# First cross attention of a two-layer block: scores by row halves of the feature axis, the maximum subtracted by VectorE, one low part by GpSimd, and a new order on every engine

## The chip, the cores and the metric

The kernel runs on one core of one Trainium2 chip. The metric is the device time of one execution in microseconds (us); a quoted time of the kernel is the median of several executions. What is shown as a row comes from one profiled execution. PE is TensorE's matmul stream and PEld its weight loads, DVE is VectorE, ACT is ScalarE, POOL is GpSimd and SP is SyncE.

## The reference, cut to what matters

The input `x` holds 64 examples of 128 tokens by 128 features, and every example has a context of 77 tokens. Two layers follow each other; each is a cross attention to the context and then a mixture of experts with 8 experts, and both parts are added to `x` times a gate. Only the first attention concerns the change. Its heads have 8 features, and a feature map makes 16 out of them:

```python
def _feature_map(x, fm_w, fm_b):
    z = jnp.einsum('nshd,ed->nshe', x, fm_w) + fm_b
    return jnp.concatenate([jnp.exp(z), jnp.exp(-z)], axis=-1)
v, k, q = (_feature_map(x, fm_w, fm_b) for x in (v, k, q))
scores = jnp.einsum('nqhd,nkhd->nhqk', q, k) / jnp.sqrt(jnp.float32(EMBED))
attn = jax.nn.softmax(scores, axis=-1)
out = jnp.einsum('nhql,nlhd->nqhd', attn, v)
out = out.reshape(N, S, HEADS * EXP_DIM)
return out @ fc_w.T + fc_b
```

The queries are the layer-normalized `x`, keys and values are the context, and there are 16 heads.

## The kernel before, in words

`flamingo_kernel` runs its stages one behind the other, with a barrier between them: loading `x` (it stays in SBUF as `x_all`), the constants of the layer norm, the first attention (`feature_attention`, the stage a0), router and experts of layer 0, the second attention (`relative_attention`, written in the same way), and router and experts of layer 1. The change is in `feature_attention` and in the call of `layernorm_constants` ahead of it.

In `feature_attention` every engine runs a loop over slots, one slot for one example n, and a slot holds steps of neighbouring examples: while the scores of example n are made, the probabilities of n-1 are multiplied with the values, and n-2 and n-3 are finished. The function `slot` of each engine is the order, written out by hand; the engines meet only at semaphores. `slots` (L62) writes the first and last slots out and loops over the middle ones, two slots in a pass.

The steps of an example, with the lines of the kernel before:

- `normalize` (L420, DVE) makes the normalized rows `a_xn`, `prep_turn` (L222, PE) transposes them, `copy_xn` (L323, ACT) copies them beside the context in `a_xc`; `prep_z` (L228, PE) and `features` (L329, ACT, the exponential) make `a_feat`, whose 256 features lie in two halves c of 128 partitions, 8 heads in each.
- POOL (L393) writes `a_kfeat`: the 77 keys of a half c eight times over, each time with all but one head's 16 partitions at zero. So one matmul over 128 partitions gives the scores of four heads, and the other heads add nothing. `add_bias` is POOL's third instruction (L401).
- A quarter u is four heads. `scores` (L248, PE) makes its 128 x 308 scores in one of two PSUM banks, in float32. `row_max` (L426, DVE) takes the maximum of each head. For quarters 0 to 2, `shift_by_max` (L432, DVE) scales the four maxima, and `exp` (L342, ACT) runs four activations, one for a head, out of PSUM with that bias. For quarter 3 (`ON_DVE`), DVE subtracts the maxima from all 308 columns (L437) and one activation follows (L346).
- `turn` (L258, PE) transposes the four heads into PSUM, `high_prob` (L354, ACT) copies them as float16, and `low_prob` (L445, DVE) subtracts that copy from the PSUM values, which leaves the low part. `mix` (L267, PE) multiplies high and low parts with the values, 12 small matmuls for a quarter. `prep_value`, `high_value` and `low_value` make the two parts of the values.
- `inverse_sum` and `divide` (DVE), `fin_turn` (PE), `copy_mixed` (ACT), `fin_project` (PE), `residual` and `statistics` (DVE) finish an example.

Two places of the code matter for the waits. The first is that `scores` waits until ACT has read the bank (L252), the second that the DVE's scaling of the maxima has SBUF on both sides:

```python
wait(pe, exped, 4 * n + u - 1)
nc.tensor.matmul(score_ps[u % 2][:, 0:QW], feat[p][:, c, 0:P],
                 kfeat[p][:, c, 4 * (u % 2):4 * (u % 2) + 4, :],
...
nc.vector.tensor_scalar(shift[u][:, :], top[u][:, :], -SCALE, None,
                        ALU.mult).then_inc(shift_ready, 1)
```

## Time and profile before

| What | Value |
| --- | --- |
| Median of 3 runs | 2408.27 us (2404.83 to 2421.33) |
| The profiled execution | 2413.15 us |
| Its span, first to last instruction | 2411.4 us |
| Mean granted TensorE clock | 0.944 of full speed |
| PE, DVE, ACT, POOL busy over the span | 92%, 86%, 67%, 64% |

The profiled execution took 4.88 us more than the median of the runs, and its span leaves 1.75 us of it outside. The stage a0 is a fifth of the span, from 31 to 534 us. A row of a timeline says when an instruction or a run of equal ones (x2, x4) starts, how long it lasts, and in brackets how long the engine sat idle before it and what it then waited for. An engine starts its next instruction before the last one has ended for good, so the time that an instruction takes out of an engine's slot is the distance from start to start, a little less than the length shown.

### The profile page before, as it was taken

How to read it: one execution, taken by the hardware profiler on the slowest of the kernel's cores; microseconds unless marked ns; L12 is line 12 of the kernel's file. 1: busy time of each engine (PE TensorE's matmuls, PEld its weight loads, DVE VectorE, ACT ScalarE, POOL GpSimd, SP SyncE). 2: the span in 40 equal slices, each digit the busy share in tenths (PEclk: the TensorE clock that was granted, in tenths of full speed). 3: DMA queues.
4: the chain of work that ended last, by engine and by line, in shares of the span. 5: the costliest groups of instructions: out<-in, count | busy, mean ns of one | idle time of the engine just before them, and what ended most of it. 6: DMA issues, size and time to landing. Idle time of an engine off the chain costs nothing. (4 is left out here: it accounts for less than half of the span.)

```text
span 2411.4 us, 83171 instructions
## 1 busy us (share of the span) xinstructions
PE 2227.9 (92%) x28294; PEld 1764.3 (73%) x28294; DVE 2070.8 (86%) x4625; ACT 1610.1 (67%) x3917; POOL 1534.7 (64%) x1166
## 2 busy tenths in 40 slices
PE   4999999978879999999999399999999986899999
PEld 3888888865546666666666299999999976566666
DVE  6999999987878888888889588888888878888888
ACT  4888888863345555565565377777777753688887
POOL 2333333324446666666666499999999953688888
PEclk9999999995589999999999699999999985899999
DMA  2000000003052222222221345555555530000000
GB/s 80 6 5 5 5 5 5 5 4 69 0 112 83 84 83 80 85 78 90 75 90 54 86 80 75 83 74 81 77 79 78 77 55 35 6 13 13 13 13 13
DMA packets 476806, 123.92 MB, mean 51 GB/s; under 512 B 431731, under 2 KB 446707, under 8 KB 475968
## 3 DMA queue, kind: packets, MB, share of 16 engines
q1 hardware_dynamic: 344352, 89.38, 17.5%
q10 hardware_dynamic: 132384, 33.63, 6.3%
q8 instruction: 41, 0.67, 0.1%
q14 instruction: 29, 0.24, 0.0%
HBM read 109.03 MB, written 13.89 MB: 51 GB/s over the span
## 5 line engine op out<-in xcount | busy, mean ns | idle before, releaser
L1086 POOL TENSOR_TENSOR f_low<-f_hidden,f_high 128x512 f16<-128x512 f32 x336 | 442.3, 1322 | 250.1 <-ACT f_high L1021 248.1
L1044 DVE TENSOR_TENSOR f_hidden<-f_hidden,f_share 128x512 f32<-128x512 f32 x336 | 374.2, 1114 | 0.0
L398 POOL TENSOR_TENSOR a_kfeat<-a_feat,a_head_mask 128x616 f32<-128x616 f32 x128 | 153.7, 1221 | 312.2 <-ACT a_feat L333 312.2
L1230 POOL TENSOR_TENSOR f_low<-f_hidden,f_high 128x512 f16<-128x512 f32 x256 | 296.6, 1159 | 70.9 <-ACT f_high L1173 70.5
L1027 ACT ACTIVATE f_act_out<-f_gate 128x512 f32<-128x512 f32 x336 | 200.4, 596 | 194.8 <-PE f_gate L991 194.8
L1067 DVE SCALAR_TENSOR_TENSOR f_hidden<-f_up,f_act_out 128x512 f32<-128x512 f32 x336 | 229.8, 684 | 82.8 <-PE f_up L991 59.6
L1615 POOL TENSOR_TENSOR a_q_head_high<-a_q_t_high,a_head_mask 128x2048 f16<-128x2048 f16 x64 | 233.0, 3640 | 56.2 <-PE a_score L1417 48.2
L1021 ACT ACTIVATE f_high<-f_hidden 128x512 f16<-128x512 f32 x336 | 210.5, 627 | 72.7 <-DVE f_hidden L1044 71.3
L1001 PE MATMUL f_y<-w_down_high,f_high 128*128 128x128 f16 x1344 | 242.6, 220 | 2.2 <-POOL f_low L1086 2.2
L1001 PE MATMUL f_y<-w_down_high,f_low 128*128 128x128 f16 x1344 | 242.6, 219 | 0.0
L1001 PE MATMUL f_y<-w_down_low,f_high 128*128 128x128 f16 x1344 | 242.5, 219 | 0.0
L1615 POOL TENSOR_TENSOR a_q_head_low<-a_q_t_low,a_head_mask 128x2048 f16<-128x2048 f16 x64 | 232.8, 3638 | 0.0
L1216 DVE SCALAR_TENSOR_TENSOR f_hidden<-f_in,f_act_out 128x512 f32<-128x512 f32 x256 | 175.7, 686 | 50.2 <-ACT f_act_out L1180 50.2
L1557 ACT ACTIVATE a_prob_t_high<-a_trans 77x512 f16<-77x512 f32 x256 | 151.6, 592 | 94.0 <-PE a_trans L1426 88.5
L350 ACT ACTIVATE a_prob<-a_score,a_shift 128x77 f32<-128x77 f32 x768 | 185.4, 327 | 40.4 <-DVE a_shift L442 32.9
L1180 ACT ACTIVATE f_act_out<-f_in 128x512 f32<-128x512 f32 x256 | 152.8, 597 | 76.2 <-PE f_in L1142 70.6
L254 PE MATMUL a_score<-a_kfeat,a_feat 128*128 128x308 f32 x512 | 192.2, 458 | 6.1 <-ACT a_prob L350 1.5
L1718 DVE TENSOR_TENSOR a_prob_t_low<-a_trans,a_prob_t_high 77x512 f16<-77x512 f32 x256 | 175.0, 684 | 17.7 <-ACT a_prob_t_high L1557 6.0
L1415 PE MATMUL a_score<-a_k_t_high,a_q_head_high 128*128 128x77 f16 x1024 | 186.5, 201 | 2.8 <-POOL a_q_head_low L1615 2.8
L1417 PE MATMUL a_score<-a_key_table_low,a_q_pos 128*128 128x77 f16 x1024 | 186.8, 202 | 0.0
L1417 PE MATMUL a_score<-a_key_table_high,a_q_pos 128*128 128x77 f16 x1024 | 186.7, 202 | 0.0
L1154 PE MATMUL f_y<-w_high,f_high 128*128 128x128 f16 x1024 | 184.9, 220 | 1.8 <-DVE x_all L1194 0.5
(264 smaller groups left out, 9025.0 us busy)
## 6 DMA issues: line engine op xcount, KB each, us to landing
f_share<-expert_shares SPq DMA_DIRECT2D x128, 256.0 KB, 3.1
a_q_pos<-queries ACTq DMA_DIRECT2D x64, 512.0 KB, 4.2
f_share<-expert_shares SPq DMA_DIRECT2D x128, 128.0 KB, 3.0
relative_values<-a_rel_all SPq DMA_DIRECT2D x512, 8.0 KB, 1.7
x_all<-in_x SPq DMA_DIRECT2D x4, 1024.0 KB, 8.0
f_share<-expert_shares SPq DMA_DIRECT2D x128, 32.0 KB, 1.8
queries<-a_q_parts SPq DMA_DIRECT2D x64, 64.0 KB, 4.3
a_rel<-relative_values SPq DMA_DIRECT2D x64, 64.0 KB, 3.6
```

The lines of the kernel that those rows point to most:

```text
L254: nc.tensor.matmul(score_ps[u % 2][:, 0:QW], feat[p][:, c, 0:P], kfeat[p][:, c, 4 * (u % 2):4 * (u % 2) + 4, :], start=True, stop=True).th ...
L350: last = nc.scalar.activation(prob[u][:, h, :], score_ps[u % 2][:, KC * h:KC * (h + 1)], ACT.Exp, bias=shift[u][:, h:h + 1], scale=SCALE)
L1001: mm = nc.tensor.matmul(dst, h[r][:, own], w_down[part][:, m, :], start=(m == 0 and t == 0 and k == 0), stop=(m == M - 1 and k == 2), skip ...
L1021: nc.scalar.activation(high[r][:, :], hidden[r][:, :], ACT.Copy).then_inc(high_ready, 1)
L1027: nc.scalar.activation(act_out[m % RING][:, :], gate_ps[m % BANKS][:, :], ACT.Silu, scale=1.0 / WSCALE).then_inc(act_ready, 1)
L1044: nc.vector.tensor_tensor(hidden[r][:, :], hidden[r][:, :], share[k][:, :, :].rearrange("p t q -> p (t q)"), ALU.mult).then_inc(scaled, 1)
L1067: nc.vector.scalar_tensor_tensor(out=hidden[r][:, :], in0=up_ps[m % BANKS][:, :], scalar=1.0 / WSCALE, in1=act_out[r][:, :], op0=ALU.mult, ...
L1086: nc.gpsimd.tensor_tensor(low[r][:, :], hidden[r][:, :], high[r][:, :], ALU.subtract).then_inc(low_ready, 1)
L1230: nc.gpsimd.tensor_tensor(low[k][:, :], hidden[k][:, :], high[k][:, :], ALU.subtract).then_inc(low_ready, 1)
L1415: nc.tensor.matmul(dst, q[:, QC * g:QC * (g + 1), :], t[:, :], start=(k == 0), stop=False)
L1417: mm = nc.tensor.matmul(dst, q_pos[p][:, g, :], key_table[k][:, 0, window], start=False, stop=(k == 1))
L1615: nc.gpsimd.tensor_tensor(q_head[p][k][:, :, :], q_t[p][k][:, :].unsqueeze(2).broadcast_to([P, P, NH]), head_mask[:, :].unsqueeze(1).broad ...
```

## The change

- **Row halves.** `scores` takes a half c instead of a quarter u. For each of the two halves r of the partitions (0 to 63 and 64 to 127, four heads in each) it issues one matmul over 64 partitions, into bank r; u is 2c + r. `a_kfeat` needs the keys four times instead of eight, with a mask `own_mask` that is the sum of the two halves of the old one.
- **Maximum.** For all four quarters DVE subtracts the maxima out of PSUM into `a_prob` (`subtract_max`), and `exp` is one activation of 128 x 308 from SBUF to SBUF. The scaling of the maxima and `shift` are gone. `scores` now waits for the subtraction (`shifted`), not for the exponential.
- **Normalizing** goes from DVE to ACT (`normalize`, scale and bias from `xn_shift`, which `layernorm_constants` now makes with one more DVE instruction).
- **Low part of quarter 3.** ACT copies the transposed quarter 3 once more, as float32, to `prob_3` (`whole_prob`), and POOL subtracts the float16 copy from it (`low_prob` on POOL). DVE keeps the other three.
- **Order.** The slot of each engine is written anew. `turn` of quarter 1 now waits for `whole_prob` and `high_prob` of quarter 3, `mix` of quarter 3 for POOL and moves to the next slot; `mask_keys` of POOL runs one example ahead and stands behind POOL's `low_prob`; `prep_turn` and `fin_turn` move from the last part of a slot to the first part of the next.

The diff, cut to its core:

```diff
-                def scores(n, p, u):
-                    if inside(n, 0, B):
-                        if u % 2 == 0:
-                            pe.wait_ge(kfeat_ready, 2 * n + u // 2 + 1)
-                        wait(pe, exped, 4 * n + u - 1)
-                        c = u // 2
-                        nc.tensor.matmul(score_ps[u % 2][:, 0:QW], feat[p][:, c, 0:P],
-                                         kfeat[p][:, c, 4 * (u % 2):4 * (u % 2) + 4, :],
-                                         start=True, stop=True).then_inc(score_ready, 1)
+                def scores(n, p, c):
+                    if inside(n, 0, B):
+                        pe.wait_ge(kfeat_ready, 2 * n + c + 1)
+                        wait(pe, shifted, 4 * n + 2 * c)
+                        for r in range(2):
+                            own = slice(HALF * r, HALF * (r + 1))
+                            nc.tensor.matmul(score_ps[r][:, 0:QW], feat[p][own, c, 0:P], kfeat[p][own, c, :, :],
+                                             start=True, stop=True).then_inc(score_ready, 1)
 
                 def turn(n, u):
                     if inside(n, 0, B):
                         pe.wait_ge(exped, 4 * n + u + 1)
-                        wait(pe, prob_low, 4 * n + u - 1)
+                        if u == 1:
+                            wait(pe, prob_3_whole, n)
+                            wait(pe, prob_high, 4 * n)
+                        else:
+                            wait(pe, prob_low, 3 * n + max(u - 1, 0))
...
                 def mix(n, p, u):
                     if inside(n, 0, B):
-                        pe.wait_ge(prob_low, 4 * n + u + 1)
+                        if u == 3:
+                            pe.wait_ge(prob_3_low, n + 1)
+                        else:
+                            pe.wait_ge(prob_low, 3 * n + u + 1)
...
                 def slot(n, p):
                     o = 1 - p
+                    mix(n - 2, p, 3)
                     scores(n, p, 0)
+                    prep_turn(n + 1, o)
+                    fin_turn(n - 3, o)
                     turn(n - 1, 2)
+                    turn(n - 1, 3)
                     prep_z(n + 1, o)
-                    mix(n - 1, o, 0)
                     fin_project(n - 3, o)
                     scores(n, p, 1)
-                    turn(n - 1, 3)
+                    mix(n - 1, o, 0)
+                    turn(n, 0)
                     prep_value(n, p)
                     mix(n - 1, o, 1)
-                    scores(n, p, 2)
-                    turn(n, 0)
+                    turn(n, 1)
                     mix(n - 1, o, 2)
-                    fin_turn(n - 2, p)
-                    prep_turn(n + 2, p)
-                    scores(n, p, 3)
-                    turn(n, 1)
-                    mix(n - 1, o, 3)
...
                 def exp(n, u):
                     if inside(n, 0, B):
-                        act.wait_ge(shift_ready, 4 * n + u + 1)
-                        if u in ON_DVE:
-                            last = nc.scalar.activation(prob[u][:, :, :], prob[u][:, :, :], ACT.Exp, scale=SCALE)
-                        else:
-                            wait(act, prob_ready, 4 * n + u - 3)
-                            for h in range(HQ):
-                                last = nc.scalar.activation(prob[u][:, h, :], score_ps[u % 2][:, KC * h:KC * (h + 1)],
-                                                            ACT.Exp, bias=shift[u][:, h:h + 1], scale=SCALE)
-                        last.then_inc(exped, 1)
+                        act.wait_ge(shifted, 4 * n + u + 1)
+                        nc.scalar.activation(prob[u][:, :, :], prob[u][:, :, :], ACT.Exp, scale=SCALE).then_inc(exped, 1)
...
+                def whole_prob(n):
+                    if inside(n, 0, B):
+                        act.wait_ge(prob_ready, 4 * n + 4)
+                        wait(act, prob_3_low, n)
+                        nc.scalar.activation(prob_3[:, :, :],
+                                             trans_ps[1][0:KC, :].rearrange("k (h q) -> k h q", h=HQ),
+                                             ACT.Copy).then_inc(prob_3_whole, 1)
...
+                def normalize(n, p):
+                    if inside(n, 0, B):
+                        wait(act, xn_t, n - 1)
+                        nc.scalar.activation(xn[p][:, :], x_all[:, n, :], ACT.Identity, bias=xn_shift[:, n, :],
+                                             scale=rstd[:, n, :]).then_inc(xn_ready, 1)
+
                 def slot(n, p):
                     o = 1 - p
+                    exp(n - 1, 3)
+                    copy_xn(n + 1, o)
+                    normalize(n + 3, o)
+                    copy_mixed(n - 3, o)
                     high_prob(n - 1, 2)
+                    exp(n, 0)
+                    whole_prob(n - 1)
+                    high_prob(n - 1, 3)
                     features(n + 1, o)
-                    exp(n, 0)
-                    high_prob(n - 1, 3)
+                    exp(n, 1)
                     high_value(n, p)
-                    exp(n, 1)
                     high_prob(n, 0)
+                    high_prob(n, 1)
                     exp(n, 2)
-                    copy_xn(n + 2, p)
-                    high_prob(n, 1)
-                    copy_mixed(n - 2, p)
-                    exp(n, 3)
...
+                def low_prob(n):
+                    if inside(n, 0, B):
+                        pool.wait_ge(prob_3_whole, n + 1)
+                        pool.wait_ge(prob_high, 4 * n + 4)
+                        nc.gpsimd.tensor_tensor(prob_t[3][1][:, :, :], prob_3[:, :, :], prob_t[3][0][:, :, :],
+                                                ALU.subtract).then_inc(prob_3_low, 1)
+
+                def mask_keys(n, p):
                     if inside(n, 0, B):
                         pool.wait_ge(feat_ready, n + 1)
                         wait(pool, score_ready, 4 * n - 4)
                         for c in range(2):
                             nc.gpsimd.tensor_tensor(
-                                kfeat[p][:, c, :, :], feat[p][:, c, P:P + KC].unsqueeze(1).broadcast_to([P, 8, KC]),
-                                head_mask[:, :].unsqueeze(2).broadcast_to([P, 8, KC]), ALU.mult).then_inc(kfeat_ready, 1)
+                                kfeat[p][:, c, :, :], feat[p][:, c, P:P + KC].unsqueeze(1).broadcast_to([P, HQ, KC]),
+                                own_mask[:, :].unsqueeze(2).broadcast_to([P, HQ, KC]), ALU.mult).then_inc(kfeat_ready, 1)
+
+                def add_bias(n):
+                    if inside(n, 0, B):
                         nc.gpsimd.tensor_tensor(x_all[:, n, :], x_all[:, n, :], fc_b[:, :],
                                                 ALU.add).then_inc(x_biased, 1)
 
-                pool.wait_ge(weights_ready, 4)
-                slots(pool, 0, LO, HI, B, slot)
+                def slot(n, p):
+                    low_prob(n - 1)
+                    mask_keys(n + 1, 1 - p)
+                    add_bias(n)
...
-                def shift_by_max(n, u):
-                    if inside(n, 0, B):
+                def subtract_max(n, u):
+                    if inside(n, 0, B):
+                        s = score_ps[u % 2][:, 0:QW].rearrange("q (h k) -> q h k", h=HQ)
                         dve.wait_ge(top_ready, 4 * n + u + 1)
-                        if u in ON_DVE:
-                            wait(dve, prob_ready, 4 * n + u - 3)
-                            nc.vector.tensor_tensor(
-                                prob[u][:, :, :], score_ps[u % 2][:, 0:QW].rearrange("q (h k) -> q h k", h=HQ),
-                                top[u][:, :].unsqueeze(2).broadcast_to([P, HQ, KC]), ALU.subtract).then_inc(shift_ready, 1)
-                        else:
-                            wait(dve, exped, 4 * n + u - 3)
-                            nc.vector.tensor_scalar(shift[u][:, :], top[u][:, :], -SCALE, None,
-                                                    ALU.mult).then_inc(shift_ready, 1)
+                        wait(dve, prob_ready, 4 * n + u - 3)
+                        nc.vector.tensor_tensor(prob[u][:, :, :], s, top[u][:, :].unsqueeze(2).broadcast_to([P, HQ, KC]),
+                                                ALU.subtract).then_inc(shifted, 1)
...
                 def slot(n, p):
                     o = 1 - p
                     row_max(n, 0)
+                    row_max(n, 1)
+                    subtract_max(n, 0)
+                    subtract_max(n, 1)
                     inverse_sum(n - 2, p)
-                    shift_by_max(n, 0)
                     low_prob(n - 1, 2)
                     divide(n - 2, p)
-                    row_max(n, 1)
                     residual(n - 3)
-                    shift_by_max(n, 1)
-                    low_prob(n - 1, 3)
-                    low_value(n, p)
                     row_max(n, 2)
                     statistics(n - 3)
-                    shift_by_max(n, 2)
+                    row_max(n, 3)
+                    subtract_max(n, 2)
+                    subtract_max(n, 3)
+                    low_value(n, p)
                     low_prob(n, 0)
-                    row_max(n, 3)
-                    normalize(n + 3, o)
-                    shift_by_max(n, 3)
                     low_prob(n, 1)
...
-        layernorm_constants(nc, "ln0", stats, mean[:, :, 0], rstd[:, :, 0], B)
-        feature_attention(nc, B, io, x_all, stats, mean, rstd, ident, gates)
+        layernorm_constants(nc, "ln0", stats, mean[:, :, 0], rstd[:, :, 0], B, xn_shift[:, :, 0])
+        feature_attention(nc, B, io, x_all, stats, mean, rstd, xn_shift, ident, gates)
```

What the new order looks like is seen best on DVE and PE. First DVE, where the rows begin a slot that is written out (example 3, ahead of the loop); `a0_score0` and `a0_score1` are the two banks, the number behind `a0_top`, `a0_shift`, `a0_prob` and `a0_prob_t` is the quarter. Before:

```order
L430 TENSOR_REDUCE a0_top0<-a0_score0 128x4
L464 RECIPROCAL a0_rden1<-a0_mix1 128x16
L442 TENSOR_SCALAR a0_shift0<-a0_top0 128x4
L449 TENSOR_TENSOR a0_prob_t2_low<-a0_trans0,a0_prob_t2_high 77x512
L471 TENSOR_TENSOR a0_mixed1<-a0_mix1,a0_rden1 128x256
L430 TENSOR_REDUCE a0_top1<-a0_score1 128x4
L479 TENSOR_TENSOR x_all<-x_all,a0_fin 128x128
L442 TENSOR_SCALAR a0_shift1<-a0_top1 128x4
L449 TENSOR_TENSOR a0_prob_t3_low<-a0_trans1,a0_prob_t3_high 77x512
L456 SCALAR_TENSOR_TENSOR a0_vfeat1_low<-a0_prep,a0_vfeat1_high 77x16x16
L430 TENSOR_REDUCE a0_top2<-a0_score0 128x4
L485 BN_STATS stats<-x_all 128x6
```

And now:

```order
L455 TENSOR_REDUCE a0_top0<-a0_score0 128x4
L455 TENSOR_REDUCE a0_top1<-a0_score1 128x4
L462 TENSOR_TENSOR a0_prob0<-a0_score0,a0_top0 128x308
L462 TENSOR_TENSOR a0_prob1<-a0_score1,a0_top1 128x308
L484 RECIPROCAL a0_rden1<-a0_mix1 128x16
L469 TENSOR_TENSOR a0_prob_t2_low<-a0_trans0,a0_prob_t2_high 77x512
L491 TENSOR_TENSOR a0_mixed1<-a0_mix1,a0_rden1 128x256
L499 TENSOR_TENSOR x_all<-x_all,a0_fin 128x128
L455 TENSOR_REDUCE a0_top2<-a0_score0 128x4
L505 BN_STATS stats<-x_all 128x6
L455 TENSOR_REDUCE a0_top3<-a0_score1 128x4
L462 TENSOR_TENSOR a0_prob2<-a0_score0,a0_top2 128x308
```

The two maxima of a pair of banks now stand together, and both subtractions follow at once where before a scaling and a low part came between; the low part of quarter 3 is no longer there.

On PE the rows begin the first slot behind the loop; the 12 matmuls of each `mix` are left out where "..." stands. Before:

```order
L254 MATMUL a0_score0<-a0_kfeat0,a0_feat0 128x308
L263 MATMUL a0_trans0<-ident,a0_prob2 77x128 x4
L235 MATMUL a0_prep<-a0_xc1,a0_fm_w 128x205 x2
...
L295 MATMUL a0_fin<-a0_fc_w,a0_mixed_t1 128x128 x2
L254 MATMUL a0_score1<-a0_kfeat0,a0_feat0 128x308
L263 MATMUL a0_trans1<-ident,a0_prob3 77x128 x4
L244 MATMUL a0_prep<-ident,a0_feat0 77x128 x2
...
L254 MATMUL a0_score0<-a0_kfeat0,a0_feat0 128x308
L263 MATMUL a0_trans0<-ident,a0_prob0 77x128 x4
```

And now:

```order
L255 MATMUL a0_score0<-a0_kfeat0,a0_feat0 128x308
L255 MATMUL a0_score1<-a0_kfeat0,a0_feat0 128x308
L227 MATMUL a0_prep<-ident,a0_xn1 128x128
L294 MATMUL a0_fin<-ident,a0_mixed1 128x128 x2
L267 MATMUL a0_trans0<-ident,a0_prob2 77x128 x4
L267 MATMUL a0_trans1<-ident,a0_prob3 77x128 x4
L236 MATMUL a0_prep<-a0_xc1,a0_fm_w 128x205 x2
L302 MATMUL a0_fin<-a0_fc_w,a0_mixed_t1 128x128 x2
L255 MATMUL a0_score0<-a0_kfeat0,a0_feat0 128x308
L255 MATMUL a0_score1<-a0_kfeat0,a0_feat0 128x308
...
L267 MATMUL a0_trans0<-ident,a0_prob0 77x128 x4
```

Before, the four scores stand apart, with at least a transposition of four heads between two of them. Now they come in two pairs, the two matmuls of a pair directly behind each other and into different banks; between the first pair and the second stand both transpositions of n-1, and the preparation of n+1.

## Rows read from the trace of the kernel before

**Rows 1.** Parts 1 and 2 of the page: busy time, then granted TensorE clock in 40 slices.

```profile
PE 2227.9 (92%) x28294; PEld 1764.3 (73%) x28294; DVE 2070.8 (86%) x4625; ACT 1610.1 (67%) x3917; POOL 1534.7 (64%) x1166
PEclk9999999995589999999999699999999985899999
```

**Rows 2.** Windows view, columns: stretch, length, PE, PEld, DVE, ACT, POOL, PEclk, DMA, GB/s.

```profile
100.00:500.00 400.00, 384.23 (x4399) 326.59 (x4398) 373.79 (x934) 339.56 (x1089) 144.43 (x156) 1.00 0.03 5
```

**Rows 3.** POOL timeline (start, length, operation): second, one later and last pair of L398.

```profile
39.76 2.40 POOL L398 TENSOR_TENSOR a_kfeat<-a_feat,a_head_mask 128x616 f32<-128x616 f32 x2 [1.95 <-ACT a_feat L333]
...
308.01 2.40 POOL L398 TENSOR_TENSOR a_kfeat<-a_feat,a_head_mask 128x616 f32<-128x616 f32 x2 [5.09 <-ACT a_feat L333]
...
515.13 2.40 POOL L398 TENSOR_TENSOR a_kfeat<-a_feat,a_head_mask 128x616 f32<-128x616 f32 x2 [4.95 <-ACT a_feat L333]
```

**Rows 4.** Timeline of DVE, slot from 308.59 to 316.49.

```profile
308.59 0.48 DVE L430 TENSOR_REDUCE a_top<-a_score 128x4 f32<-128x308 f32 x1 [0.41 <-PE a_score L254]
308.98 0.28 DVE L479 TENSOR_TENSOR x_all<-x_all,a_fin 128x128 f32 x1
309.19 1.24 DVE L442 TENSOR_SCALAR a_shift<-a_top 128x4 f32<-128x4 f32 x1
310.35 0.68 DVE L449 TENSOR_TENSOR a_prob_t_low<-a_trans,a_prob_t_high 77x512 f16<-77x512 f32 x1
310.95 0.41 DVE L456 SCALAR_TENSOR_TENSOR a_vfeat_low<-a_prep,a_vfeat_high 77x256 f16<-77x256 f32 x1
311.28 0.46 DVE L430 TENSOR_REDUCE a_top<-a_score 128x4 f32<-128x308 f32 x1
...
316.49 0.48 DVE L430 TENSOR_REDUCE a_top<-a_score 128x4 f32<-128x308 f32 x1 [0.33 <-PE a_score L254]
```

**Rows 5.** Timeline of PE, slot from 246.12 to 253.32.

```profile
246.12 0.68 PE L254 MATMUL a_score<-a_kfeat,a_feat 128*128 128x308 f32 x2
246.64 0.60 PE L263 MATMUL a_trans<-ident,a_prob 128*77 128x128 f32 x4
...
250.73 0.79 PE L254 MATMUL a_score<-a_kfeat,a_feat 128*128 128x308 f32 x2
251.35 0.60 PE L263 MATMUL a_trans<-ident,a_prob 128*77 128x128 f32 x4
...
253.32 0.68 PE L254 MATMUL a_score<-a_kfeat,a_feat 128*128 128x308 f32 x2
```

**Rows 6.** Groups by shape, 100 to 500 us: count, busy us, mean ns, idle before.

```profile
L350 ACT ACTIVATE a_prob<-a_score,a_shift 128x77 f32<-128x77 f32 x623 | 150.5, 327 | 35.3 <-DVE a_shift L442 29.4 <-PE a_trans L263 5.9
L358 ACT ACTIVATE a_prob_t_high<-a_trans 77x512 f16<-77x512 f32 x207 | 123.5, 597 | 22.0 <-PE a_trans L263 16.8
L254 PEld LDWEIGHTS a_score<-a_kfeat,a_feat 128*128 128x128 f32 x414 | 62.1, 190 | 9.3 <-ACT a_prob L350 7.1 <-issue 0.2
L346 ACT ACTIVATE a_prob<-a_prob 128x308 f32<-128x308 f32 x52 | 25.0, 481 | 0.0
L442 DVE TENSOR_SCALAR a_shift<-a_top 128x4 f32<-128x4 f32 x156 | 69.0, 442 | 0.0
L423 DVE TENSOR_SCALAR a_xn<-x_all,mean,rstd 128x128 f32 x52 | 17.3, 332 | 0.0
```

**Rows 7.** Single lines over the whole run: count, ns min/median/max, first and last start.

```profile
L442 DVE TENSOR_SCALAR a_shift<-a_top x192: 116/170/1243, 38.2 to 525.5; 128x4 f32<-128x4 f32 x192
L1711 DVE TENSOR_TENSOR a_prob<-a_score,a_top x256: 455/471/480, 1385.5 to 1970.6; 128x308 f32<-128x308 f32 x128
L1718 DVE TENSOR_TENSOR a_prob_t_low<-a_trans,a_prob_t_high x256: 669/686/689, 1390.5 to 1974.1; 77x512 f16<-77x512 f32 x128
L1544 ACT ACTIVATE a_xn<-x_all,xn_shift,rstd x64: 478/486/495, 1371.6 to 1936.7; 128x128 f32 x56, 128x128 f32<-128x128 f32 x8
```

**Rows 8.** Part 5 of the page: POOL groups outside the first attention.

```profile
L1230 POOL TENSOR_TENSOR f_low<-f_hidden,f_high 128x512 f16<-128x512 f32 x256 | 296.6, 1159 | 70.9 <-ACT f_high L1173 70.5
L1615 POOL TENSOR_TENSOR a_q_head_high<-a_q_t_high,a_head_mask 128x2048 f16<-128x2048 f16 x64 | 233.0, 3640 | 56.2 <-PE a_score L1417 48.2
```

32 lines of the change are left out of this document (16 added, 16 removed).

## The prediction, made before the changed kernel ran

> **What bounds the kernel now.** I read the page first. Over the whole span PE is the busiest engine at 92%, with DVE at 86% [rows 1], but these are averages over stages that the change doesn't touch. So I cut the first attention out with the windows view. In 400 us of its middle PE is busy for 384, DVE for 374, ACT for 340 and POOL for 144 us, at the full granted clock of 1.00, the level of 2.4 GHz [rows 2]. Two engines are nearly full, and a busy PE isn't PE at its peak, so busy time can't say which of them sets the pace. The length of a slot can.
>
> POOL's mask pair comes once per slot. From the second to the last there are 62 distances and 515.13 - 39.76 = 475.37 us, so a slot takes 7.67 us on average [rows 3]. Behind the first few, no slot takes 7.67: in the timeline they last either 7.89 or 7.20 us. The long kind is the DVE timeline from 308.59 to 316.49 [rows 4], the short kind the PE timeline from 246.12 to 253.32 [rows 5]. What makes the difference is the scaling of the maxima, L442. Its median is 0.17 us, its longest 1.24 [rows 7]. The long one starts at 309.19 while POOL's pair runs from 308.01 to 310.41, and the next DVE instruction starts at 310.35 [rows 3, 4]: DVE stands still until POOL's two multiplications are through. In slots where it happens to miss them, the slot takes 7.20 us, and DVE has room.
>
> In such a short slot PE hardly waits: I find about 0.1 us. So there are two limits, one close above the other: PE at 7.1 to 7.2 us of work per slot, and in most slots a DVE that is held up by POOL and drags PE to 7.89.
>
> **What the change does to DVE.** Per slot DVE is busy 373.79 / 52 = 7.19 us (the 156 scalings of the window are three for each of 52 slots) [rows 2, 6]. Gone are the three scalings, 69.0 / 52 = 1.33 us with their stall; one of four low parts, 0.60 from start to start (310.35 to 310.95) [rows 4]; and the normalizing, 0.33 less the usual overlap of 0.07, 0.26 [rows 6]. Added are three subtractions of 128 x 308. The same instruction in the second attention takes 0.47 us [rows 7], as long as a maximum of 0.48, of which 0.39 stay from start to start [rows 4]; so 3 x 0.39 = 1.17. The sum is 7.19 - 1.33 - 0.60 - 0.26 + 1.17 = 6.17 us.
>
> Can the stall come back in another instruction? POOL's new load is two masks of half the width, 1.2 us for both, a low part of 77 x 512 at about 1.16 us (128 x 512 from float32 to float16 takes 1.159, [rows 8]) and the bias, some 2.8 us, about what it has now (144.43 / 52 = 2.78, [rows 2]). But the DVE instructions that stay read at most one operand from SBUF and the other from PSUM. In the second attention POOL works in pieces of 3.64 us [rows 8] beside just these instructions, and the subtraction never takes over 0.480 nor the low part over 0.689 us [rows 7]. I cost contention at nothing; if it came back at its old price it would be 1.07 us in a slot, and DVE would be at 7.24.
>
> **ACT.** It is busy 339.56 / 52 = 6.53 us per slot [rows 2]. The twelve small exponentials go, 150.5 / 52 = 2.89; three large ones come at 0.48, one whole copy at 0.60 like its neighbour and the normalizing at 0.49 [rows 6, 7]. That is 6.53 - 2.89 + 1.44 + 0.60 + 0.49 = 6.17 us as an upper bound, since lengths overlap. It doesn't bind, but the slack below a slot of 6.6 is small.
>
> **PE.** Here the trace of before doesn't show what is decisive: two float32 matmuls over 64 partitions each, one behind the other. A score matmul over 128 partitions takes 0.52 to 0.62 us from start to start [rows 5], and it is two MATMUL records (x2). I take 0.57, so four scores are 2.28 and the rest of a short slot is 7.20 - 2.28 = 4.92 us. For a new pair there are these bounds.
>
> - Lower bound: the halves run wholly beside each other, a pair costs one score, 0.57. PE is at 4.92 + 1.14 = 6.06.
> - Upper bound without side effects: no overlap, a pair costs 1.14 and PE stays at 7.20.
> - Upper bound with side effects, from the nearest rows: each change between half-height and full-height matmuls lets the array run empty. A score lasts 0.79 where the next instruction starts after 0.62 [rows 5], so the tail is 0.17, and four changes in a slot are 0.68: PE at 7.88.
>
> I take a value between the first two: PE issues in order, and a pair is four records, low half twice and then high half twice. Only the second and the third belong to different halves and can run side by side, so a pair costs three quarters of 1.14, 0.85. PE is then at 4.92 + 1.70 = 6.62.
>
> The Trainium skill, TensorEngine Tiling (Array Packing), Theoretical Speedup, gives up to 2x for a contraction of 64 or less; by it a pair would be at the lower bound and PE at 6.06. No row here shows it. The same page, Key Properties, says that a change of tiling mode drains TensorE, which speaks against the change; by that rule some of the four tails would be paid. No row here shows that either.
>
> **How the engines meet.** The new order gives DVE two maxima in a row and then both subtractions, so an instruction no longer waits for its own predecessor's result. From the first maximum of a slot to the third DVE has 4 x 0.39 and the small ones and one low part, about 2.9 us. On PE half of the 4.92 us and one pair lie between the two pairs, 2.45 + 0.85 = 3.30. So DVE waits some 0.35 us at the third maximum and would come to 6.17 + 0.35 = 6.52, a little below PE. The new waits fall like this. POOL's low part can start when ACT's copies of quarter 3 are done, about the middle of the slot, and ends 1.2 us later; behind it in POOL's queue are the masks for the next example, 0.6 us to the first one that a score needs. That leaves more than 0.5 us before the next slot. `mix` of quarter 3 was put off by a slot for it. `turn` of quarter 1 waits for two ACT copies that are issued some 1.5 us ahead of it. I cost these waits at nothing.
>
> **The sum.** A slot of 6.62 instead of 7.67 us saves 62 x 1.05 = 65.1 us. The added DVE instruction ahead of the stage costs about 0.2, and the start and the end of the stage stay as they are within some 3 us. Against the profiled execution that is 2413.15 - 65.1 + 0.2 = 2348 us. The profiled execution took 4.88 us more than the median of the runs, so I forecast 2344 us for the median.
>
> **Rivals.**
>
> - Full overlap. PE at 6.06, DVE sets the pace at 6.17 with a wait of some 0.1 at the third maximum: 6.3 us, 62 x 1.37 = 85 saved, 2324 us. For it: the halves use different partitions and banks. Against it: the order of the records.
> - No overlap. PE stays at 7.20 in all slots; only the stall goes, 62 x 0.47 = 29 saved, 2379 us. For it: nothing in this trace shows two matmuls at once. With all four tails a slot is 7.88, and the time is 13 us above now, 2421.
> - Slower: no overlap, the tails, and weight loads that can't be hidden. It decides at the score pairs on PE. Loads take 0.19 us each [rows 6] and run beside matmuls today. If the eight loads of the four half matmuls stood in the open, that is 1.52 more, a slot of 9.40, 62 x 1.73 = 107 lost, 2516 us; above 8.06 us a slot costs over 1%. The Trainium skill, TensorE: Matmul & The Clock Gate, Part 3 (The mechanism), says that a load is only pulled ahead where the rows differ or it goes to the background buffer; the loads here run ahead with equal rows, so I give this rival little.
> - The change doesn't do what it says: another wait (ACT at 6.17 with its order, or POOL's low part ahead of the masks) holds every slot at 7.1 or more. Then it is 2373 or above, near the case without overlap.
>
> **Chances.** Half overlap 0.42, full overlap 0.27, no overlap or another wait near 7.1 to 7.2 together 0.21, with tails near no change 0.06, clearly slower 0.04. The likeliest is 2344. A range that leaves out 2 in 10 goes from a little below full overlap to a little above the case without overlap, 2314 to 2386. About 1% (24 us) is what a measurement of this kernel can tell from no change: faster by more (under 2384) 0.86, within it 0.09, slower 0.05.
>
> **What would show it.** In the changed trace POOL's first mask should come every 6.6 us; a distance of 6.2 to 6.3 is the full overlap, 7.2 none. The second half matmul of a pair should start about 0.3 us behind the first for half overlap. No DVE instruction of the stage should last over 0.7 us. At the third maximum DVE should wait for PE. I am wrong in kind if a slot exceeds 7.2 us, if POOL's low part is what PE waits for, or if the granted clock of the stage falls below 1.00 because PE stands idle more often; in the stretches between the stages the clock reads 5 tenths, the level of 1.2 GHz [rows 1].

## The result, and the profile after

| | before | after |
|---|---|---|
| median of the runs, us | 2406.55 (4 runs, 2400.47 to 2421.33) | 2337.49 (4 runs, 2334.19 to 2339.66) |
| profiled execution, us | 2413.15 | 2339.3 |
| its span, us | 2411.4 | 2337.4 |
| mean slot of the first attention, us | 7.67 | 6.43 |

The ratio after to before is 0.9703, 95% interval 0.9657 to 0.9750. In the profiled executions 73.9 us are gone. Parts 1 and 2 of the page after, against [rows 1]:

```profile
PE 2164.1 (93%) x28294; PEld 1706.1 (73%) x28294; DVE 2009.8 (86%) x4499; ACT 1556.1 (67%) x3469; POOL 1541.5 (66%) x1230
PEclk9999999855899999999998799999999975999999
```

PE has as many instructions as before. Where the time went is read from three rows: `mean<-stats` (L104) is DVE's first instruction behind the first attention, behind the first mixture and behind the second attention. First the DVE timeline of before, then that of after:

```profile
535.22 0.27 DVE L104 TENSOR_TENSOR mean<-stats 128x64 f32<-128x64 f32 x1 [0.91 <-PEq L511]
1346.19 0.27 DVE L104 TENSOR_TENSOR mean<-stats 128x64 f32<-128x64 f32 x1 [0.31 <-PEq L966]
1988.31 0.27 DVE L104 TENSOR_TENSOR mean<-stats 128x64 f32<-128x64 f32 x1 [0.31 <-PEq L1339]
```

```profile
457.53 0.27 DVE L104 TENSOR_TENSOR mean<-stats 128x64 f32<-128x64 f32 x1 [0.92 <-PEq L528]
1267.08 0.27 DVE L104 TENSOR_TENSOR mean<-stats 128x64 f32<-128x64 f32 x1 [0.31 <-PEq L983]
1914.53 0.27 DVE L104 TENSOR_TENSOR mean<-stats 128x64 f32<-128x64 f32 x1 [0.31 <-PEq L1356]
```

The first attention ends 77.7 us earlier. The mixture takes 809.5 instead of 811.0 us. The second attention takes 647.5 instead of 642.1, a difference without a change in its code; over the profiles of the experiments it lies between 641.6 and 649.7. So the whole gain is in the first attention, and the next rows are about its slots. The windows view of 100 to 420 us, against [rows 2], columns as there:

```profile
100.00:420.00 320.00, 320.00 (x4236) 269.71 (x4235) 310.24 (x799) 284.46 (x700) 143.38 (x200) 1.00 0.03 6
```

The window holds 50 slots. PE is busy all the time, DVE for 6.20 us per slot, ACT for 5.69 and POOL for 2.87, at a granted clock of 1.00. POOL's second and last mask pairs (start, length, operation), against [rows 3]:

```profile
41.06 1.36 POOL L419 TENSOR_TENSOR a_kfeat<-a_feat,a_own_mask 128x308 f32<-128x308 f32 x2 [4.02 <-ACT a_feat L338]
...
439.60 1.36 POOL L419 TENSOR_TENSOR a_kfeat<-a_feat,a_own_mask 128x308 f32<-128x308 f32 x2
```

There are 62 distances in 398.54 us, 6.43 us each; they alternate between 6.51 and 6.32. From 7.667 to 6.428 is 1.239 us, times 62 is 76.8: the slots alone explain the gain. "Slot" below always means this mean over 62 distances. One slot on PE (start, length, operation), against [rows 5]:

```profile
299.95 0.79 PE L255 MATMUL a_score<-a_kfeat,a_feat 64*128 64x308 f32 x4
300.67 0.33 PE L227 MATMUL a_prep<-ident,a_xn 128*128 128x128 f32 x1
...
303.16 0.79 PE L255 MATMUL a_score<-a_kfeat,a_feat 64*128 64x308 f32 x4
303.88 0.18 PE L283 MATMUL a_mix<-a_vfeat_high,a_prob_t_high 77*128 77x17 f16 x1
```

A pair (four records, two score quarters) holds PE for 0.72 us up to the next instruction's start; a single full-height quarter took 0.52 to 0.62 in [rows 5]. The single records of the trace start at 303.159, 303.166, 303.523 and 303.530: they come in couples, 7 ns apart. And the same slot on DVE, against [rows 4]:

```profile
303.13 0.41 DVE L491 TENSOR_TENSOR a_mixed<-a_mix,a_rden 128x256 f32<-128x256 f32 x1
303.46 0.27 DVE L499 TENSOR_TENSOR x_all<-x_all,a_fin 128x128 f32 x1
303.98 0.48 DVE L455 TENSOR_REDUCE a_top<-a_score 128x4 f32<-128x308 f32 x1 [0.24 <-PE a_score L255]
304.38 0.28 DVE L505 BATCH_NORM_STATS2 stats<-x_all  x1
304.58 0.46 DVE L455 TENSOR_REDUCE a_top<-a_score 128x4 f32<-128x308 f32 x1
304.95 0.85 DVE L462 TENSOR_TENSOR a_prob<-a_score,a_top 128x308 f32<-128x308 f32 x2
```

No DVE instruction of the stage lasts over 0.69 us, and in this slot its one wait is at the third maximum, for PE. The waits of 100 to 420 us, all above 5 us (total, times, longest):

```profile
POOL a_prob_t_low L411 <- ACT a_prob_t_high L356: 176.6, 50, 3.6
ACT a_vfeat_high L345 <- PE a_prep L245: 24.0, 50, 0.5
PEld a_prep L227 <- issue: 20.9, 50, 0.4
PEld a_mix L283 <- issue: 20.9, 50, 0.4
ACT a_xc L332 <- PE a_prep L227: 12.1, 50, 0.3
DVE a_top L455 <- PE a_score L255: 6.5, 28, 0.2
```

The two rows with "issue" are the weight loads of the first full-height (or 77-row) instruction behind each pair. They wait 0.4 us twice per slot, for nothing that the profile shows. The loads of before have one such row in the same window, in some slots only:

```profile
PEld a_prep L226 <- issue: 7.2, 13, 0.6
```

### The profile page after: what moved, and what is told of

It is laid out like the page before. It is cut to its first block and busy times, and to the rows that moved or that the text cites. A ratio compares the mean times of both kernels' runs of the same rounds, so it can differ in the third digit from the quotient of the medians.

```text
span 2337.4 us, 82626 instructions
## 1 busy us (share of the span) xinstructions
PE 2164.1 (93%) x28294; PEld 1706.1 (73%) x28294; DVE 2009.8 (86%) x4499; ACT 1556.1 (67%) x3469; POOL 1541.5 (66%) x1230
## 5 line engine op out<-in xcount | busy, mean ns | idle before, releaser
L411 POOL TENSOR_TENSOR a_prob_t_low<-a_prob,a_prob_t_high 77x512 f16<-77x512 f32 x64 | 73.9, 1155 | 226.9 <-ACT a_prob_t_high L356 223.0
L1432 PE MATMUL a_score<-a_k_t_high,a_q_head_low 128*128 128x77 f16 x1024 | 187.1, 202 | 0.0
L1432 PE MATMUL a_score<-a_k_t_low,a_q_head_high 128*128 128x77 f16 x1024 | 186.8, 202 | 0.0
```

What stands on the lines that cost most here:

```text
L1432: nc.tensor.matmul(dst, q[:, QC * g:QC * (g + 1), :], t[:, :], start=(k == 0), stop=False)
```

## The experiments

The change has three parts that can each act: DVE is freed from the stall and given other work, the order is new, and the scores run by halves. The runs below remove or add one at a time. The ratio of each is to the kernel before, measured on the same chip. The chips differ: before took 2396.59 us on that of e1, e2, e3 and e7, 2407.58 on that of e4, e5 and e6, and 2413.64 on that of e8 to e11. So the medians of two rows can be compared only where they share a chip. The slot of before, 7.67, comes from a profiled execution of 2413.15 us.

| run | what it is | median us | ratio, 95% interval | slot us |
|---|---|---|---|---|
| before | | | | 7.67 |
| e3 | before, maxima in PSUM | 2386.47 | 0.9961 (0.9940 to 0.9981) | 7.17 |
| e2 | before, all four quarters subtracted by DVE | 2373.30 | 0.9896 (0.9870 to 0.9922) | 7.01 |
| e9 | e2, the bank freed by the subtraction, and the moves to ACT and POOL, old order | 2394.88 | 0.9917 (0.9887 to 0.9947) | 7.38 |
| e7 | before and halves alone | 2471.88 | 1.0314 (1.0285 to 1.0342) | 8.22 steady |
| e1 | after with full-height scores | 2368.01 | 0.9873 (0.9850 to 0.9897) | 6.90 |
| after | | 2337.49 | 0.9703 (0.9657 to 0.9750) | 6.43 |
| e4 | after, second pair twice in a row | 2370.14 | 0.9845 (0.9774 to 0.9916) | 6.95 |
| e11 | after, extra pair standing apart | 2397.52 (one run) | | 7.33 |
| e5 | after, low part of quarter 3 on DVE | 2350.37 | 0.9762 (0.9716 to 0.9809) | 6.62 |
| e6 | after, normalizing on DVE | 2360.17 | 0.9803 (0.9756 to 0.9850) | 6.76 |
| e8 | after, loop unrolled by four | 2375.73 | 0.9849 (0.9813 to 0.9884) | 6.43 |
| e10 | before once more | 2414.66 (one run) | | 7.68 |

### e3: is the long slot of before a DVE held up by POOL?

```diff
-    nc.vector.tensor_reduce(top[u][:, :], s, AX_X, ALU.max)
+    nc.vector.tensor_reduce(top_ps(u), s, AX_X, ALU.max)   # quarters 0 to 2: a PSUM column
-    nc.vector.tensor_scalar(shift[u][:, :], top[u][:, :], -SCALE, None,
+    nc.vector.tensor_scalar(shift[u][:, :], top_ps(u), -SCALE, None,
```

> The kernel before with nothing changed but the place of twelve numbers in a slot: the maxima of quarters 0 to 2 lie in free columns of the score bank in PSUM instead of in SBUF, so that the small scaling instruction on DVE reads PSUM. Theory A, the scaling is held up because it and POOL's mask both want SBUF: no scaling lasts over 0.4 us, all slots take 7.2 us, the time is about 62 x 0.47 = 29 us below the kernel before. Rival D, the 1.24 us are a wait for something else (a semaphore, a register): the long scalings stay, slots of 7.89 us stay, and the time doesn't move.

The group of the scaling, 100 to 420 us, against L442 of [rows 6] with its mean of 442 ns:

```profile
L445 DVE TENSOR_SCALAR a_shift<-a_score 128x4 f32<-128x4 f32 x133 | 21.6, 162 | 0.0
```

The same operation, in the same place beside the same POOL work, takes 162 ns once its input is in PSUM. Behind the first few, the slots are 7.12 to 7.27 us; the 7.89 kind is gone. So it is the scaling from SBUF to SBUF that is held up beside POOL, and in the two profiles the stall was worth 0.49 us per slot. The Trainium skill, SBUF — State Buffer, Who interferes with whom, says that a tensor_scalar can enter a mode of DVE that takes the pair of ports shared with GpSimd, and that whichever of the two comes later is then blocked until the other ends. The trace agrees: 1.24 us beside POOL, 0.16 with one end in PSUM.

The whole time moved less. 62 x 0.49 is 31 us, and on its own chip e3 is 10 us faster than before (2386.47 against 2396.59). e1 and e2, on the same chip, also gain 17 to 19 us less there than their slots give against 7.67. Before was therefore faster on that chip than in its profile; whether fewer of its slots were long there isn't known, because no profile of before was taken on it. So 0.49 us is the price of the stall in the profiled execution of before, and the median on e3's chip shows a third of it.

### e2: DVE subtracts in all quarters, nothing else

```diff
-        ON_DVE = (3,)
+        ON_DVE = (0, 1, 2, 3)
```

> The kernel before with one part of the change alone: DVE subtracts the maximum for all four quarters and each exponential is one activation; order, whole-height scores, POOL and normalizing as before. Theory A, two limits (PE at 7.2 us per slot, and the scaling of the maxima that is held up by POOL's masks): with no scaling left, DVE is at 7.19 - 1.33 + 1.17 = 7.03 us, the 7.89 us slots vanish and PE's 7.2 stays, so a slot is 7.2 to 7.3 us, and the time some 25 us (1%) below the kernel before, about 2380. Rival C, DVE's work bounds the slots of before and the stall only fills time in which it would wait: a slot stays at 7.6 to 7.9 us and the time within 5 us of before.

The slot is 7.01 us (7.03 in the steady part), below the 7.20 that I had taken for PE's own work and had expected here. The order, the operands and the number of matmuls on PE are those of before. So 7.20 was not PE's work: about 0.2 us of it was waiting that PE's busy time doesn't show, since the length of a record reaches beyond the start of the next (in e3, at 7.20 us, PE counts as busy for 319.58 of 320 us). DVE is full here, at the 7.03 us that its work had been summed to, so 7.01 is again only an upper bound for PE. The windows view of 100 to 420 us, where DVE (third number pair) has no idle time:

```profile
100.00:420.00 320.00, 320.00 (x3871) 282.35 (x3870) 320.00 (x820) 240.46 (x546) 127.87 (x137) 1.00 0.03 6
```

### e9: the moves to ACT and POOL, but in the old order

```diff
-        ON_DVE = (3,)
+        ON_DVE = (0, 1, 2, 3)
...
-                    low_prob(n - 1, 3)      # DVE
-                    normalize(n + 3, o)     # DVE
+                    whole_prob(n - 1)       # ACT
+                    normalize(n + 3, o)     # ACT
+                    low_prob(n - 1)         # POOL, behind the bias
```

> The kernel before with the rest of the change but neither row halves nor the new order: maximum subtracted by DVE for all quarters, normalizing on ACT, low part of quarter 3 by POOL from ACT's whole copy, bank freed by the subtraction; the order of before kept (whole copy ahead of the float16 one, POOL's low part behind the bias). Against the run with all but the halves in the new order (6.90 us) it shows what the order is worth, against all-subtract alone (7.01) what the two moves are worth. If PE's matmuls need about 6.9 us and the order isn't what limits: 6.9 to 7.0 us, about 2370 us. If the new order carries a good part: 7.1 us or more, 2380 us or more.

Scores wait for the subtraction here, as in after. The moves take work from the full engine of e2, and the slot still grows from 7.01 to 7.38. Three of its waits, 100 to 420 us, 43 slots:

```profile
ACT a_prob L375 <- PE a_trans L269: 36.2, 43, 0.8
DVE a_vfeat_low L483 <- ACT a_vfeat_high L349: 31.7, 43, 0.7
ACT a_prob L355 <- DVE a_prob L464: 25.7, 44, 0.6
```

ACT stands 0.8 us per slot at the whole copy with other copies queued behind it, and DVE 0.7 us for one of them. Moving work off a full engine cost time here until the order was made for it. Against e1, which does the same work in the new order, the new order is worth 7.38 - 6.90 = 0.48 us per slot.

### e1: after, with scores over the full height

```diff
-    own = slice(HALF * r, HALF * (r + 1))
-    nc.tensor.matmul(score_ps[r][:, 0:QW], feat[p][own, c, 0:P], kfeat[p][own, c, :, :],
+    own = slice(HQ * r, HQ * (r + 1))
+    nc.tensor.matmul(score_ps[r][:, 0:QW], feat[p][:, c, 0:P], kfeat[p][:, c, own, :],
```

The masks are again 616 wide.

> The changed kernel with one part undone: each score matmul again takes all 128 partitions and four of eight masked heads (mask of 128 x 616 on POOL), two of them directly behind each other as in the new order. All else as changed. Theory A, the row halves run beside each other (a pair now takes 0.72 us of PE, two whole scores 2.28 in four, that is 1.14 a pair): a slot goes from 6.42 to 6.42 + 2 x 0.42 = 7.26 us, and the time from 2337 to about 2337 + 62 x 0.84 = 2389 us. Rival B, the halves bring nothing and the new order and the missing stall brought all: a slot stays within 0.1 us of 6.42, the time at 2337 to 2343 us.

The slot is 6.90, between the two expectations: halves are worth 0.47 us per slot, 29 us in all. A pair over the full height, timeline of PE:

```profile
306.01 1.28 PE L255 MATMUL a_score<-a_kfeat,a_feat 128*128 128x308 f32 x4
307.13 0.27 PE L227 MATMUL a_prep<-ident,a_xn 128*128 128x128 f32 x1
```

It holds PE for 1.12 us, near my 2 x 0.57. With 2 x 1.12 for the scores, the rest of PE's slot is at most 6.90 - 2.24 = 4.66 us, not 4.92.

### e4 and e11: what is a pair, and what is a change of height?

In e4 the second pair is issued twice in a row; in e11 the second issue stands between full-height instructions, ahead of `fin_project`. Both issue one redundant pair per slot.

```diff
+                        for r in range(2 * c):      # e4: in scores(n, p, 1), again
+                            own = slice(HALF * r, HALF * (r + 1))
+                            nc.tensor.matmul(score_ps[r][:, 0:QW], feat[p][own, c, 0:P], kfeat[p][own, c, :, :],
+                                             start=True, stop=True)
...
+                    extra_pair(n, p)                # e11: the same two matmuls, earlier in the slot
```

> The changed kernel with the second pair of score matmuls issued twice in a row (the first time for nothing: the same values into the same banks). PE is full in the changed kernel, so the slot grows by what a pair costs inside a run of half-height matmuls, with no change of height added. If the halves run wholly beside each other: +0.52 us, a slot of 6.94, +32 us. If only the second and third of four records overlap: +0.77, a slot of 7.19, +48 us. If they don't overlap: +1.03, 7.45, +64 us. What is left of the 0.72 us of a pair after that is the price of two changes of height.

> The changed kernel with the second pair of score matmuls issued once more for nothing, as in the run with the pair twice in a row, but ahead of the output projection, so that whole-height matmuls stand on both sides of it. The difference between this slot and that of the pair twice in a row (6.95 us) is the price of going to half height and back once. Theory A' (halves overlap wholly at 0.52 us a pair, and a change of height costs about 0.15 us each way): a slot of 6.43 + 0.52 + 0.3 = 7.25 us. If a change of height costs nothing and something else lengthens the pairs: 6.95 us again.

e4's slot is 6.951, longer than after's by 0.523 us. That is a pair inside a stretch of half-height matmuls: two quarters in the time of one. In PE's timeline the two stand 0.62 us apart, with the way into the half-height stretch in the first of them; inside the stretch the couples of records follow each other after 0.259 us, as long as a single full-height record takes in e1. A half without a neighbour has its two records 0.36 us apart (e7), so a couple is one record of each half:

```profile
303.73 0.79 PE L255 MATMUL a_score<-a_kfeat,a_feat 64*128 64x308 f32 x4
304.35 0.69 PE L259 MATMUL a_score<-a_kfeat,a_feat 64*128 64x308 f32 x4
```

e11's slot is 7.325. The extra pair costs 0.897 us when it stands apart, so a change to half height and back costs 7.325 - 6.951 = 0.374 us, where 0.3 was expected. The waits of e11 name the place: a third load now waits 0.4 us on "issue", that of the instruction behind the extra pair.

```profile
PEld a_prep L227 <- issue: 18.4, 44, 0.4
PEld a_mix L292 <- issue: 18.0, 43, 0.4
PEld a_fin L311 <- issue: 18.0, 43, 0.4
PEld a_score L264 <- DVE a_prob L472: 10.9, 44, 0.2
```

The last row is a rival: the extra pair may also have waited for DVE's subtraction. It didn't lengthen the slot in the stretch at 302 us. There the pair starts 0.265 us behind the record before it, 0.09 more than the usual step of 0.17 between such records, and the pair at 303.16 us in after, without that wait, also starts 0.09 us more than the usual step behind its predecessor (0.204 against 0.109).

This closes the sum. After: two pairs of 0.52, two changes of 0.37 and a rest give 6.43, so the rest is 4.64; e1 gives at most 4.66 for the same rest by another way. The halves gain 1.20 us (2.24 - 1.04) and give 0.75 back. The Trainium skill, TensorEngine Tiling (Array Packing), Key Properties, says that a change of the tiling mode drains TensorE. The runs fit that, at 0.37 us for a change and its return.

### e7: halves without the pairing

Before, with its old order, where each quarter's score is a single matmul between full-height ones. The masks shrink as in the change.

```diff
-    nc.tensor.matmul(score_ps[u % 2][:, 0:QW], feat[p][:, c, 0:P],
-                     kfeat[p][:, c, 4 * (u % 2):4 * (u % 2) + 4, :],
+    own = slice(HALF * (u % 2), HALF * (u % 2 + 1))
+    nc.tensor.matmul(score_ps[u % 2][:, 0:QW], feat[p][own, c, 0:P], kfeat[p][own, c, :, :],
```

> The kernel before with row halves alone, in the old order: every score is one matmul over 64 partitions, but the four of a slot stand apart with whole-height work between them, and POOL's mask is half as wide. So there are eight changes of height in a slot and never two halves side by side. Theory A (halves only pay as neighbours; a change of height costs PE about 0.1 us, as two of them and 0.52 us of scores make the 0.72 of a pair): PE goes from 7.2 to 7.2 + 8 x 0.1 = 8.0 us per slot less what single scores already wasted, 7.6 to 8.0, the time near or above the kernel before, 0 to +20 us, although the stall of the scaling gets shorter (a mask pair of 1.4 us). Rival E, a matmul over 64 partitions is itself cheaper, with or without a neighbour: a slot falls under 7.2 us and the time by over 30 us.

The steady slot is 8.22, above the 7.6 to 8.0 that I expected: a single half holds PE for 0.71 us (from 303.29 to 304.00 below), as long as the 0.72 of a pair, and PE goes to half height and back four times in a slot. With the rest of 4.64, four scores of 0.57 and four changes of 0.37 this would be 8.40; measured 8.22. Halves lose unless two run together. The waits of 100 to 420 us show the four returns:

```profile
PEld a_trans L263 <- issue: 64.0, 153, 0.4
```

There is a second loss, which nobody had expected. The first slots took 10.71, 12.89, 13.42, 14.36 and 14.36 us. Timeline of PE at 66 us, 107 us and 303 us:

```profile
66.07 1.39 PE L255 MATMUL a_score<-a_kfeat,a_feat 64*128 64x308 f32 x2
67.39 1.14 PE L263 MATMUL a_trans<-ident,a_prob 128*77 128x128 f32 x4
...
106.80 0.66 PE L263 MATMUL a_trans<-ident,a_prob 128*77 128x128 f32 x4
...
303.29 0.78 PE L255 MATMUL a_score<-a_kfeat,a_feat 64*128 64x308 f32 x2
304.00 0.66 PE L263 MATMUL a_trans<-ident,a_prob 128*77 128x128 f32 x4
```

Until 106 us the same instructions take some 1.75 times as long, both kinds; from start to start a transposition takes 0.213 us instead of 0.109. The windows view of 60 to 110 us shows 1.00 as the granted clock:

```profile
60.00:110.00 50.00, 50.00 (x318) 35.59 (x318) 24.60 (x66) 24.25 (x77) 7.09 (x12) 1.00 0.02 4
```

This 1.00 isn't a measurement. The trace's first record of the granted clock in e7, at 1.00, begins at 106.2 us, and the view counts a stretch without a record as full. In the other profiles that first record begins between 39.4 and 44.3 us. After shows the same step there: its transpositions take 0.213 us up to 43.0 us and 0.109 from 45.0 on, and its record begins at 44.3. So durations and records agree that TensorE was granted half of its full speed, the level of 1.2 GHz, until 106.2 us, although PE counts as busy in all of the 50 us shown. By the slots above 8.22 this costs about 25 us: the six distances from 10.71 to 8.78 sum to 74.5, less 6 x 8.22. Of the 75 us by which e7 is slower than before, 50 remain without it. Why the clock rose so late in this kernel alone stays open.

### e5 and e6: was it right to take these two from DVE?

e5 puts the low part of quarter 3 back on DVE and drops the whole copy and POOL's low part. e6 puts the normalizing back on DVE, behind the last subtraction.

```diff
-                    whole_prob(n - 1)                   # e5, ACT
-                    low_prob(n - 1)                     # e5, POOL
+                    low_prob(n - 1, 3)                  # e5, DVE, at the end of its slot
...
-                    normalize(n + 3, o)                 # e6, ACT
+                    normalize(n + 3, o)                 # e6, DVE, behind subtract_max(n, 3)
```

> The changed kernel with the low part of quarter 3 back on DVE, behind the residual, and without ACT's whole copy and POOL's subtraction. DVE gets 0.60 us more on 6.2. Theory A, PE at 6.41 us sets the pace and DVE has 0.2 us of room: a slot of 6.8 to 6.9, bound by DVE, +24 to +30 us. Rival F, DVE had more room than that, or ACT's and POOL's extra steps cost as much as they save: a slot stays under 6.5 us and the time within 5 us of the changed kernel.

> The changed kernel with the normalizing back on DVE (float32 from SBUF to SBUF with two scalars), between the last subtraction and the low part of the values, a time at which POOL is at its masks. Without contention DVE is at 6.2 + 0.26 = 6.46 us and a slot takes about 6.5, +5 us. With the contention of the scaling in the kernel before, the normalizing is held up until POOL's run of instructions ends, up to about 1 us: a slot of 6.8 to 7.4 us, +25 to +60 us, and single normalizing instructions of over 0.8 us in the trace.

In both, DVE has no idle time left (320.00 us of 320). In e5 0.60 us of work come back and the slot grows by 0.20 to 6.62, between the two expectations, so after had 0.40 us of room on DVE. In e6 0.26 us of work come back, which would fit into that room, and the slot grows by 0.33 to 6.76. DVE and then POOL in e6:

```profile
305.50 0.81 DVE L447 TENSOR_SCALAR a_xn<-x_all,mean,rstd 128x128 f32 x1
306.23 0.41 DVE L475 SCALAR_TENSOR_TENSOR a_vfeat_low<-a_prep,a_vfeat_high 77x256 f16<-77x256 f32 x1
```

```profile
304.87 1.35 POOL L412 TENSOR_TENSOR a_kfeat<-a_feat,a_own_mask 128x308 f32<-128x308 f32 x2
```

The normalizing, 0.332 us before [rows 6], starts while POOL's masks run and is through just when they end, at 306.22. Its mean over 47 slots is 812 ns. It is the old stall in another instruction: held up, it takes 0.73 us of DVE from start to start, which less the room of 0.40 is the growth of 0.33. Moving it to ACT keeps it away.

Not every DVE instruction with all its operands in SBUF is held up. The statistics in after (L505, from `x_all` to `stats`, both in SBUF) start while POOL works in every slot from 60 to 450 us, and take 0.279 to 0.286 us; beside an idle POOL in before they took 0.272 to 0.280. Only the two instructions of the form TENSOR_SCALAR were seen to wait.

### e8: unrolling, and e10: before again

e8 runs the loop of the first attention four slots at a time.

```diff
-        with eng.Fori(0, (hi - lo) // 2) as i:
-            for r in range(2):
+        with eng.Fori(0, (hi - lo) // 4) as i:
+            for r in range(4):
```

> The changed kernel with four slots in a pass of the loop instead of two. In the changed kernel slots alternate between 6.51 and 6.33 us. If the longer one holds the loop's branch, half of the 0.18 us is saved every second slot: 62 x 0.045 = 3 us off, about 2334 us. If the alternation comes from something else: no difference.

The first attention doesn't change: slot 6.43, L104 at 457.39 instead of 457.53. The kernel is slower all the same, and the place is the mixture behind it, whose code is the same. Its end in e8, on DVE, against 1267.08 above:

```profile
1303.78 0.27 DVE L104 TENSOR_TENSOR mean<-stats 128x64 f32<-128x64 f32 x1 [0.31 <-PEq L995]
```

It takes 846.4 instead of 809.5 us. The waits of PE's loads there are:

```profile
PEld f_gate L1018 <- issue: 23.3, 9, 3.9
PEld f_y L1030 <- issue: 12.9, 18, 1.9
```

Together they are 36 us; after has one such row, f_gate with 4.5 us in 2 waits. So these waits make 32 of the 37 us lost. No instruction of another engine releases them. The trace shows what else happens there. Part 3 of the page lists the DMA queues that carry instructions (packets, MB, share). Queue 8 has 41 packets in after, and in e8:

```profile
q8 instruction: 97, 1.59, 0.3%
```

In after no block of 16 KB comes over this queue between 756 and 1300 us: the loop of the mixture runs without it. In e8 the blocks keep coming to the end of the mixture, and at each of its six long stands of PE, some 88 us apart, one block is fetched within 0.5 us of the stand's beginning (at 763.5 us for the one of 3.6 us that ends at 766.5) and another for the shorter stand behind it (at 767.9). The granted clock falls with them, to a mean of 0.66 here:

```profile
766.00:776.00 10.00, 8.12 (x44) 4.24 (x45) 3.36 (x4) 2.70 (x5) 2.31 (x2) 0.66 0.26 64
```

So PE most likely waits for instructions that are loaded anew in each pass. Why they are loaded anew in this kernel, whether by the length or the place of the code in front, no run tested. The expected saving of 3 us didn't come in the first attention either.

> The kernel before, unchanged, profiled once more. The theory that a scaling on DVE is held up or not depending on whether it happens to meet POOL's masks says that slots of 7.2 and 7.89 us are mixed anew in each execution, and that this mix is why its times spread over 1% (2393 to 2421 us) while the changed kernel's spread over 0.2%: the number of long slots should differ from the first profile and the span with it, at 0.69 us a slot.

The idea was that the varying mix of 7.20 and 7.89 slots makes before's spread. The short slots came in other places, but there were 16 of them against 17 in the first profile, with a mean slot of 7.683 against 7.667 and nearly the same time. So the number of short slots hardly differed, the idea is neither borne out nor refuted, and the spread of before stays open.

## Why the prediction was right, and where it wasn't

The forecast was 2344 us, the measurement 2337.49; the slot 6.62 against 6.43. (By its own terms the sum is 2413.15 - 65.1 + 0.2 - 4.88 = 2343.4, a slip of less than 1 us.) By its own steps:

- **The stall of L442.** The mechanism was right, and so is the size in the profiles. e3 removed it alone: 7.67 to 7.17, where I had taken 0.47 for it. The median on e3's chip fell by 10 us only, not 29.
- **DVE at 6.17 us.** Right: 6.20. No DVE instruction of the stage lasts over 0.7 us, so contention at nothing was right too, and e6 shows the price if one instruction of the wrong form had stayed, 0.33 us per slot. The reason that I gave was too simple: the statistics read SBUF alone and still aren't held up.
- **ACT at 6.17 as an upper bound.** It is 5.69.
- **A pair at 0.85 on PE.** The size was right: 0.52 and a share of the change, 0.37, are 0.90. The mechanism was wrong, and that the size came out is luck. I had said "only the second and the third belong to different halves and can run side by side" and had costed the changes at nothing. The runs show a full overlap (e4) and a change that is paid every time (e4 to e11). The sign that I had named says the same: the second half's first record should have started 0.3 us behind the first, and it starts 7 ns behind. Two errors cancelled. The upper bound for the changes, four tails of 0.17 or 0.68 us per slot, was near the truth of 0.75; I had a number for it and gave it to the rival instead of the sum.
- **The rest at 4.92.** This is the mis-sized term and carries the miss. I took PE's work from a slot in which PE "hardly waits", 7.20 less four scores. e2 ran the same matmuls at 7.01, and e1 in the new order at 6.90. The rest is 4.64 us; 0.28 of my 4.92 wasn't PE's work. With e1's 4.66 and two pairs of 0.90 the slot is 6.45.
- **DVE waits 0.35 at the third maximum.** It waits there in each slot and nowhere else, 0.24 in the slot shown and 0.20 on average (320.00 less 310.24, over 50 slots).
- **New waits at nothing.** Right in this order, and only in it: e9 has the same moves in the old order and loses 0.36 us per slot. The order, which I gave no price of its own, is worth 0.48.
- **The rivals.** Full overlap, to which I had given 0.27, did occur on PE, but a slot of 6.3 didn't follow, because the changes of height were paid as well. Halves slower than before is what e7 shows, for halves that stand alone; in pairs each change serves two quarters.
- **PE or DVE.** PE sets the pace after: 0.52 us more on PE costs 0.52 (e4), while 0.60 more on DVE costs 0.20 (e5).

The whole time gained less than the slots: 76.8 us in the slots of the two profiles, 69 us between the medians (65 and 64 were forecast). In slots, step by step: 7.67 before, 7.17 without the stall, 7.01 with all subtractions on DVE, 7.38 with the moves, 6.90 in the new order, 6.43 by halves. The alternation of 6.51 and 6.32 in after is left open; unrolled by four it became 6.51, 6.32, 6.41 and 6.41.

## What to carry to other kernels

Don't take the shortest slot of a trace for an engine's work: change something else and see whether it goes below, as e2 did at the cost of one line. When matmuls are split by rows, price the change of height once per group, 0.37 us here, against the 0.60 us that a pair saves, and put as many halves as possible next to each other. A TENSOR_SCALAR on DVE from SBUF to SBUF, the form that was seen held up here, belongs where POOL is quiet, in another engine, or with its input in PSUM; and work that is moved off a full engine pays only once the order of the receiving engines is made for it.

## What the runs showed of the hardware

- Two float32 matmuls of 64 rows, on different halves and PSUM banks, overlap wholly although the kernel issues them one behind the other: 0.52 us for both (e4), with their records starting in couples 7 ns apart. A half without a neighbour holds PE for 0.71 us, a pair for 0.72 (e7, after).
- A change to half height and back costs 0.37 us, with a 0.4 us wait on "issue" at the next full-height load (e11, e7).
- A TENSOR_SCALAR of 128x4 from SBUF to SBUF on DVE takes 0.17 us, up to 1.24 beside POOL and 0.16 with its input in PSUM (before, e3); one of 128x128 takes 0.33 and 0.81 (before, e6). Statistics from SBUF to SBUF stay at 0.28 beside POOL (after).
- In e7 the granted clock rose to 1.00 at 106.2 us, in the other profiles between 39.4 and 44.3. Where no record of the clock exists, the view shows 1.00; the distance between transpositions, 0.213 against 0.109 us, tells the two levels apart.
- A stage whose code is unchanged became 37 us longer when a loop ahead of it was unrolled (e8), with PE's loads waiting on "issue" for up to 3.9 us while blocks of instructions were fetched, 97 on that queue in place of 41. Why they were fetched anew is open.
